# An embedding lookup and interaction tower on one core: tables laid out by partition, grams transposed straight from PSUM, and a new order of steps

## What is computed

```python
e = jnp.stack([tbl_0[ids[:, 0]], ..., tbl_25[ids[:, 25]]], axis=1)      # (512, 26, 128)
all_emb = jnp.concatenate([bottom_output[:, None, :], e], axis=1)       # (512, 27, 128)
gram = jnp.einsum('bfd,bgd->bfg', all_emb, all_emb)
z = gram[:, _TRIU_I, _TRIU_J]                                           # 351 pairs
h = jnp.concatenate([z, bottom_output], axis=1)
h = jnp.maximum(h @ W_top1 + b_top1, 0.0)                               # 479 -> 512
h = jnp.maximum(h @ W_top2 + b_top2, 0.0)                               # 512 -> 256
y = h @ W_top3                                                          # 256 -> 1
```

## Time and profile before

| | us |
|---|---|
| median of 3 runs | 102.84 (102.78 to 103.25) |
| profiled execution, first to last instruction | 100.5 |
| TensorE (PE) busy | 95.8, 95% |
| weight loads (PEld) busy | 83.0, 83% |
| VectorE (DVE) busy | 66.4, 66% |
| ScalarE (ACT) busy | 58.1, 58% |
| GpSimd (POOL) busy | 60.6, 60% |

### The profile page before, as it was taken

How to read it: one execution, slowest core, us unless ns; L and a number is a source line. 1 busy time by engine, 2 the same in 40 slices (tenths; PEclk the granted TensorE clock), 3 DMA queues, 4 the chain that set the end, 5 groups by cost and what they waited for, 6 DMA issues and landing times.

```text
span 100.5 us, 3571 instructions
## 1 busy us (share of the span) xinstructions
PE 95.8 (95%) x1512; PEld 83.0 (83%) x1512; DVE 66.4 (66%) x164; ACT 58.1 (58%) x97; POOL 60.6 (60%) x64
## 2 busy tenths in 40 slices
PE   3999999999999999999999998999999999899992
PEld 3798687888888888888979987889989989798980
DVE  2499999999999999989797009206630681078001
ACT  5556959958996999994945304352433345312341
POOL 2678777787787787777777777777777700000000
DMA  2999979999999999999982221222222200000000
GB/s 46 265 267 263 198 222 243 227 224 232 217 193 216 231 233 232 221 219 245 252 249 85 52 59 52 59 59 52 59 59 52 62 26 7 0 7 0 1 7 0
DMA packets 6544, 13.55 MB, mean 135 GB/s; under 512 B 2076, under 2 KB 2860, under 8 KB 6528
## 3 DMA queue, kind: packets, MB, share of 16 engines
q1 hardware_dynamic: 4536, 9.51, 40.6%
q0 software_dynamic: 1824, 3.74, 15.6%
q10 hardware_dynamic: 168, 0.07, 0.3%
HBM read 13.30 MB, written 0.01 MB: 132 GB/s over the span
## 4 chain that ended last, share of the span: by engine, by line
PE 86%; DMA 5%; ACT 3%; SPq 2%; issue 1%; ACTq 0%
PE acc L663 34%; PE acc L729 12%; PE acc L763 12%; PE acc L691 8%; PE ring L703 6%; PE ring L774 5%; DMA raw<-tbl 5%; PE acc L754 4%; SPq L299 2%; PE ring L737 1%; PE ring L787 1%; ACT hi L376 1%; PE ring L798 1%; ACT onehot L420 1%; ACT emb L461 1%
## 5 line engine op out<-in xcount | busy, mean ns | idle before, releaser
L359 POOL DMA_INDIRECT rows<-tbl,ids_sb x57 | 59.9, 1050 | 18.7 <-issue 17.1
L547 DVE TENSOR_SCALAR onehot<-far 125x512 fp32r<-125x512 f32 (+2 forms) x92 | 32.2, 408 | 1.6 <-ACT far L390 1.6
L663 PE MATMUL acc<-onehot,hi 125*128 125x512 f32 (+1 forms) x84 | 23.8, 406 | 0.2 <-ACT onehot L420 0.2
L663 PE MATMUL acc<-onehot,lo 125*128 125x512 f32 (+1 forms) x84 | 22.3, 390 | 0.0
L663 PEld LDWEIGHTS acc<-onehot,lo 125*128 125x128 f32 x84 | 16.1, 193 | 3.0
L663 PEld LDWEIGHTS acc<-onehot,hi 125*128 125x128 f32 x84 | 15.5, 195 | 3.7 <-DVE onehot L547 0.6
L533 DVE TENSOR_TENSOR lo<-raw,hi 125x512 fp32r<-125x512 f32 (+1 forms) x24 | 16.8, 701 | 0.6 <-ACT hi L376 0.5
L568 DVE COPY gram<-acc 128x432 f32<-128x432 f32 x4 | 3.7, 915 | 19.8 <-PE acc L729 19.8
L376 ACT CAST hi<-raw 125x1024 fp32r<-125x1024 f32 (+1 forms) x11 | 12.0, 1090 | 7.0 <-DMA raw<-tbl 2.9
L729 PE MATMUL acc<-emb 128*27 128x27 f32 x1024 | 12.6, 193 | 0.9 <-ACT emb L461 0.4
L729 PEld LDWEIGHTS acc<-emb 128*27 128x27 f32 x1024 | 10.7, 104 | 3.4 <-issue 1.4
(11 more groups left out here) (53 smaller groups left out, 84.2 us busy)
## 6 DMA issues: line engine op xcount, KB each, us to landing
raw<-tbl SPq DMA_DIRECT2D x9, 448.0 KB
raw<-tbl SPq DMA_DIRECT2D x2, 560.0 KB
ids_b<-ids SPq DMA_DIRECT2D x4, 256.0 KB, 10.5
rows<-tbl,ids_sb POOLq DMA_INDIRECT x57, 8.3
w1z<-w SPq DMA_DIRECT2D x3, 234.0 KB
w_sb<-w SPq DMA_DIRECT2D x1, 512.0 KB
raw<-tbl SPq DMA_DIRECT2D x9, 52.0 KB
raw<-tbl SPq DMA_DIRECT2D x2, 224.0 KB
```

Source lines behind the costliest of these rows:

```text
L359: nc.gpsimd.indirect_dma_start(out=rows[:, t, slot, :], out_offset=None, in_=tables[table], in_offset=bass.IndirectOffsetOnAxis(ap=ids_sb[ ...
L547: ins = nc.vector.tensor_scalar(onehot[:, n % OH_RING, k, of], far[:, t % FAR_RING, of], float(c), None, ALU.is_equal)
L663: mm = nc.tensor.matmul(acc[:, look_bank(t), 0:looked_up(t)], part_of[:, t % HL_RING, c * D:(c + 1) * D], onehot[:, n % OH_RING, k, 0:look ...
```

## The change

Two changes at once.

Tables. The host hands each small table over in a new layout: row c x 128 + p of the table stands on partition p as chunk c (128 partitions, padded with repeated rows to 1024 or 1280). far becomes |id - p| in ScalarE's one operation, so the one-hot of chunk 0 is relu(1 - far), one operation and no `away`; chunk c > 0 is where far equals 128 c. ScalarE makes chunk 0 for every table but the first, and chunk 1 too for tables 1 and 2 (`SECOND`), that one over |far - 128|. A table is one DMA, and table 2's load is issued after table 0 has landed.

Grams. The two copies to SBUF are gone: VectorE transposes from the two PSUM banks that hold a tile's products, with a stride of 27 elements. `pairs` has two buffers; a tile's first gram waits until both transposes of the tile before have read the banks (`pairs_ready`). Two banks hold grams, four layer 1. `ORDER` is new behind the lookups: nine runs of grams in place of twelve, and other places for bottom, turn, l1 and columns.

```diff
-KP = 125
+KP = 128
-GPS = 3
-TOP = 3
+GPS = 2
+TOP = 4
+SECOND = (1, 2)
...
-    return GPS + (n + 1) % TOP
+    return GPS + (n + 2) % TOP
...
-    return 0 < j < NL - 2 and (paired(j) or j >= FIRST)
+    return 0 if j == 0 else 2 if j in SECOND else 1
...
-                table = tables[LOOKED_UP[j]].rearrange("(p k) d -> p (k d)", k=chunks(j))
-                for p0, p1 in ((0, SPREAD), (SPREAD, KP)):
-                    sp.dma_start(raw[p0:p1, j % RAW_RING, c0 * D:c1 * D],
-                                 table[p0:p1, c0 * D:c1 * D]).then_inc(landed, 16)
+                table = looked[j]
+                sp.dma_start(raw[:, j % RAW_RING, c0 * D:c1 * D], table[:, c0 * D:c1 * D]).then_inc(landed, 16)
...
             load_rows(1, 0, chunks(1), raw_in[1])
+            sp.wait_ge(raw_in[0], 16)
             load_rows(2, 0, chunks(2), raw_in[2])
...
-                nc.scalar.activation(far[:, j % FAR_RING, 0:looked_up(j)], of, ACT.Identity,
-                                     bias=neg_row[:, c:c + 1]).then_inc(far_ready, 1)
+                nc.scalar.activation(far[:, j % FAR_RING, 0:looked_up(j)], of, ACT.Abs,
+                                     bias=neg_row[:]).then_inc(far_ready, 1)
...
-                        nc.scalar.activation(away[:], far[:, t % FAR_RING, :], ACT.Abs).then_inc(away_ready, 1)
...
-                        nc.scalar.activation(onehot[:, n % OH_RING, 0, :], away[:], ACT.Relu,
+                        nc.scalar.activation(onehot[:, n % OH_RING, 0, :], far[:, t % FAR_RING, :], ACT.Relu,
+                                             bias=1.0, scale=-1.0).then_inc(oh_act, 1)
+                    if 0 < t < HL_RING:
+
+                        split(t)
+                    if by_act(t) > 1:
+                        if SECOND.index(t):
+
+                            act.wait_ge(oh_act, act_made(t))
+                        nc.scalar.activation(away[:], far[:, t % FAR_RING, :], ACT.Abs,
+                                             bias=neg_second[:]).then_inc(away_ready, 1)
+                        act.wait_ge(away_ready, SECOND.index(t) + 1)
+                        nc.scalar.activation(onehot[:, n % OH_RING, 1, :], away[:], ACT.Relu,
                                              bias=1.0, scale=-1.0).then_inc(oh_act, 1)
...
-                    nc.vector.tensor_copy(gram[:, t % 2, :, UNIT:2 * UNIT].rearrange("p g u -> p u g"),
-                                          acc[:, gram_bank(t, 1), 0:UNIT * NF].rearrange("p (u g) -> p u g", g=NF)
-                                          ).then_inc(cut_dve, 1)
...
-                    nc.vector.transpose(pairs[:, 0:NF - 1, :], gram[:, t % 2, 1:NF, :]).then_inc(pairs_ready, 1)
-                    nc.vector.transpose(pairs[:, NF - 1:, :], gram[:, t % 2, 0:DELTAS, :]).then_inc(pairs_ready, 1)
+                    grams = acc[:, 0:UNITS, 0:UNIT * NF].rearrange("p n (u g) -> p g n u", g=NF)
+                    nc.vector.transpose(pairs[:, t % 2, 0:NF - 1, :].rearrange("p g (n u) -> p g n u", n=UNITS),
+                                        grams[:, 1:NF]).then_inc(pairs_ready, 1)
+                    nc.vector.transpose(pairs[:, t % 2, NF - 1:, :].rearrange("p g (n u) -> p g n u", n=UNITS),
+                                        grams[:, 0:DELTAS]).then_inc(pairs_ready, 1)
...
+                            pe.wait_ge(pairs_ready, 2 * t)
```

and of the list, its last lines:

```diff
-              ("turn", 3, 3), ("bottom", 2, 0), ("pairs", 2, 0), ("gram", 3, (0, 20)), ("bottom", 2, 1), ("l1", 2, 0),
-              ("l1", 2, 1), ("gram", 3, (20, 32)), ("l1", 2, 2), ("l1", 2, 3), ("l2", 2, 0), ("bottom", 3, 0),
+              ("l2", 1, 0), ("turn", 3, 2), ("bottom", 2, 1), ("turn", 3, 3), ("pairs", 2, 0), ("gram", 3, (0, 20)),
+              ("l1", 2, 0), ("l1", 2, 1), ("l1", 2, 2), ("gram", 3, (20, 32)), ("l1", 2, 3), ("l2", 2, 0),
```

More of the change, by code:

```diff
@@ L172, in by_act, with tower @@
 def by_act(j):
-    return 0 < j < NL - 2 and (paired(j) or j >= FIRST)
+    return 0 if j == 0 else 2 if j in SECOND else 1
 def act_made(j):
-    return sum(by_act(i) for i in range(j + 1))
+    return sum(by_act(i) for i in range(j))
 def turn_count(t, g):
     return TURNS * t + g + 1
-def tower(nc, bottom, ids, ids_t, ids_16, tables, w1, b1, w2, b2, b2_row, w3, w3_row, out):
+def tower(nc, bottom, ids, ids_t, ids_16, tables, looked, w1, b1, w2, b2, b2_row, w3, w3_row, out):
     ctx = ExitStack()
@@ L201, in tower @@
             pass
-        gram = sb("gram", [128, 2, NF, U])
-        pairs = sb("pairs", [128, NF - 1 + DELTAS, QP])
+        pairs = sb("pairs", [128, 2, NF - 1 + DELTAS, QP])
         zt = sb("zt", [ZK, 2, ZC, LANES])
@@ L370, in split @@
                     each = chunks(0) // 2 * D
-                    act.wait_ge(raw_in[0] if half else first_raw_in, 32)
+                    act.wait_ge(raw_in[0] if half else first_raw_in, 16)
                     part = slice(half * each, (half + 1) * each)
@@ L471, in _ @@
                                    ).then_inc(emb_turned, 1)
-                elif step == "gram":
-                    if not part[0] < UNIT <= part[1]:
-                        continue
-                    if t >= 2:
-                        act.wait_ge(pairs_ready, 2 * (t - 1))
-                    act.wait_ge(gram_done, t * UNITS + 1)
-                    nc.scalar.copy(gram[:, t % 2, :, 0:UNIT].rearrange("p g u -> p u g"),
-                                   acc[:, gram_bank(t, 0), 0:UNIT * NF].rearrange("p (u g) -> p u g", g=NF)
-                                   ).then_inc(cut_act, 1)
                 elif step == "pairs":
@@ L543, in _ @@
                             dve.wait_ge(oh_used, n - OH_RING + 1)
-                        for k in range(1 if by_act(t) and half == 0 else 0, chunks(t) // 2):
+                        for k in range(by_act(t) if half == 0 else 0, chunks(t) // 2):
                             c = half * chunks(t) // 2 + k
                             of = slice(0, looked_up(t) if t < NL - 2 else PART)
-                            ins = nc.vector.tensor_scalar(onehot[:, n % OH_RING, k, of], far[:, t % FAR_RING, of], float(c),
+                            ins = nc.vector.tensor_scalar(onehot[:, n % OH_RING, k, of], far[:, t % FAR_RING, of], float(KP * c),
                                                           None, ALU.is_equal)
@@ L579, in _ @@
                         dve.wait_ge(pairs_done, t)
-                    start = pairs[:, 0, 0:1]
+                    start = pairs[:, t % 2, 0, 0:1]
                     picked = bass.AP(start.tensor, start.offset, [list(start.ap[0]), [QP + 1, NF], [QP, DELTAS]])
@@ L834 @@
     ids_16_d = nc.dram_tensor("ids_16", (NL, B), I16, kind="Internal").ap()
-    tables_d = [given(f"tbl_{i}", inputs[f"tbl_{i}"]) for i in range(TABLES)]
+    tables_d = {i: given(f"tbl_{i}", inputs[f"tbl_{i}"]) for i in GATHERED + LOOKED_UP[:1]}
+    looked_d = []
+    for j, i in enumerate(LOOKED_UP):
+        table = np.asarray(inputs[f"tbl_{i}"])
+        table = table[np.minimum(np.arange(KP * chunks(j)), table.shape[0] - 1)]
+        looked_d.append(given(f"looked_{i}", table.reshape(chunks(j), KP, D).transpose(1, 0, 2).reshape(KP, -1)))
     w1_d = given("w1", w1[order])
```

82 lines of the change are left out of this document (32 added, 50 removed), and 7 rows, old and new, of the table behind.

## The result

The changed kernel takes 101.61 us (median of 20 runs, 101.02 to 102.39), the kernel before 102.59 on the same chip; the ratio is 0.9916 (95% interval 0.9895 to 0.9937), 0.86 us faster by the ratio and 0.98 by the medians. Medians are of all executions; ratios and intervals leave out those more than 1.5% above the fastest of their kernel, which are three of six of `grams_only`, its profiled one among them, three of eleven of `old_order` and at most two of any other. The profiled execution spans 100.2 us against 100.5.

A forecast was written before the change was run, and what follows sets the result against it. The prediction took TensorE as the bound, with GpSimd's gathers right behind. It took 0.7 us up to turn (3,3) and 0.8 behind it, gave 0.1 back, and forecast 102.84 - 1.4 = 101.5 us, 8-in-10 range 101.0 to 102.9.

The forecast's parts named there:

- Startup: First table lookups on TensorE: 0 to 0.7 us won by 17.7, then lost waiting for gathers at turn (0,1); 0.1 taken.
- ScalarE costs nothing: During the lookups: nothing charged for ScalarE's changed one-hot work, since it has gaps and its operations fall from 16 to 15.
- Gram runs and stalls: TensorE's grams before turn (3,3): nine runs for twelve at 0.26 each, -0.8 us; half the 1.1 us of stalls gone, -0.5.
- L461: TensorE's wait for ScalarE's copy ahead of gram 1: hidden by steps now placed between them, -0.4 us.
- the bottom steps: Both bottom steps of tile 2 move ahead of turn (3,3), 0.45 us each: +0.9 us before that turn.
- T: Start of turn (3,3), which reads the last gathers: 82.19 before, forecast 81.5, 0.7 us sooner (0.4 to 1.1).
- three switches fewer: Part of a gram run's cost: 0.19 us extra for passes ahead of a gram, saved in three runs.
- The gathers: GpSimd's last gather lands at 81.4 after 0.15 us gained from fewer VectorE operations, slightly later than TensorE's 81.3.
- the second rival: Gram stalls don't shrink, or grow, so TensorE and not the gathers sets turn (3,3), at 82.2 or later: 102.2; chance 0.1.
- From T to the end: Turn (3,3) to the end: 15.84 us falls to about 15.1, -0.8, from bottom steps moved and a gram copy dropped.
- The disputed price: VectorE's transposes reading PSUM 27 elements apart: taken as today, 1.05 and 0.57 us; upper bound 1.0 us more per tile.
- rival 1: Strided PSUM reads by VectorE's transposes cost 2.1 ns an element, 1.0 us exposed in tile 3: 102.5; chance 0.2.

The follow-up runs named there:

- grams_only: The gram part and the new step list alone, tables as in the kernel before: 102.96 us over six executions, ratio 0.9891 from three of them.
- old_order: The changed kernel with the kernel before's list of steps put back, table part and PSUM transposes kept: 102.31 us, ratio 0.9924 to the kernel before.
- cut_runs: The changed kernel with its two runs of 160 gram passes cut into 80 and 80, other steps between: 101.15 us, ratio 0.9842.
- tables_only: The table part alone, grams and step list as in the kernel before: 102.64 us, ratio 0.9983.
- after_again: The changed kernel run once more, nothing altered, for a second profile and a comparison in the same stretch of runs: 101.72 us.
- bottom_back: The changed kernel with one pair of bottom passes (tile 2, second half) behind turn (3,3) in place of ahead of it: 101.35 us, ratio 0.9874.
- shifted: The changed kernel with two of three warm-up products replaced by 32 tiny ones, moving later TensorE instructions along the stream: 106.24 us, ratio 1.0317.
- padded: The changed kernel with 112 waits on a long-set semaphore (56 instructions) ahead of TensorE's first product: 112.25 us.

## Why the prediction came out, and which steps failed

The time, 101.61 for 101.5, and the sign are right; half of the working is not, and part of the match is luck. The forecast took 1.34 us off a median of 102.84; the measured gain is 0.86 to 0.98, and the kernel before came out at 102.59.

**Startup** (up to 0.7 won by 17.7, absorbed at turn (0,1), 0.1 taken). Nothing was won in this profile, and for a reason that I had not priced: table 2, whose load waits for table 0, landed at 11.6. In the five profiles in which it landed by 10.8, turn (0,0) came at 16.8 to 16.9, so the 0.7 and a little more were won there. And the absorption is wrong: turn (0,1) never waits, so where the start gained, it was passed on (turn (0,1) at 21.8 in `cut_runs`).

**ScalarE costs nothing.** Wrong by 0.3 to 0.5 us: the one-hot of the last table came late for its part step (0.98 us for four passes in place of 0.64 in the changed kernel's profile, a wait of 0.5 in `tables_only`). And at the start TensorE waits 0.6 for the second one-hot of table 2.

**Gram runs and stalls** (-0.8 and -0.5). This is the step that failed. The gram passes of tiles 0 to 2 take 10.9 us in the seven runs of the changed kernel (the rows above) and 10.05 in the ten of before, six of which are these (the other four, of 64 and 32 passes, take 0.77, 0.42, 0.74 and 0.42):

```profile
55.43 1.15 PE L729 MATMUL acc<-emb 128*27 128x27 f32 x96
...
58.62 1.53 PE L729 MATMUL acc<-emb 128*27 128x27 f32 x96
...
66.57 1.78 PE L729 MATMUL acc<-emb 128*27 128x27 f32 x128
...
70.49 1.10 PE L729 MATMUL acc<-emb 128*27 128x27 f32 x96
...
74.16 1.19 PE L729 MATMUL acc<-emb 128*27 128x27 f32 x96
...
77.69 0.95 PE L729 MATMUL acc<-emb 128*27 128x27 f32 x64
```

Runs without a stall of 160, 128, 96, 64 and 32 passes take 1.53, 1.27, 1.00, 0.73 and 0.42; against these the stalls are 3.2 us after and 1.75 before (the waits view, which lists only part of them, has 2.1 and 1.4 for all four tiles). The three runs fewer were real, and the stalls took 1.4 more where I had taken 0.5 less. I had counted runs and not asked what a run costs that outlasts the supply of instructions. The page of the profile put them down to "issue", which I took for something that fewer runs would lessen.

**L461** (-0.4) and **the bottom steps** (+0.9): right. In all, turn (0,1) to T took 60.15 us in place of 59.48, where I had 0.8 less. These terms (0.9 for the gram passes, -0.4, +0.9, 0.3 for the part step) would give 1.7 more and not 0.7: some 1 us went outside the gram passes, where I had three switches fewer at 0.19, and no row takes it apart.

**The gathers.** The last was issued at 78.67 (78.9 forecast, 79.08 before), but T was TensorE's, as the second rival has it. The agreement proves little: in `after_again`, the same kernel, the last was issued at 79.03, and in `bottom_back`, with the same work on VectorE, at 77.82. The forecast had called 0.3 us real by the Trainium skill's rule on VectorE's and GpSimd's port (SBUF - State Buffer, the section on its two separate sides), and 0.4 came; no run takes it apart.

**From T to the end** (-0.8): -0.83. Turn to gram -0.10, gram 3 with what lies between its runs -0.09, last gram to pairs 3.62 to 2.69 (2.68 forecast), pairs to l1 +0.11, l1 to l3 with columns +0.18 (0.15 forecast). That T was late took nothing from it. But misses cancel in this sum. Gram 3's stretch was to grow by 0.2 (an l1 step of 0.67 more, a bottom step of 0.45 less) and shrank by 0.1, as the stall at place 2754 was 0.3 shorter in this profile than in that of before. Against it, turn to gram and pairs to l1 each took 0.1 more than forecast.

**The disputed price.** 1.05 and 0.57 us, the lower bound: a stride of 27 elements in PSUM costs a VectorE transpose nothing. The Trainium skill, Advanced Engine Details and Errata, section Memory Cachelines, would have every two consecutive elements together, and by it rival 1 (1.0 us more in each tile); for this operation the trace does not agree.

The profiles alone would say -0.2 at the last layer; the runs say -0.86. Each timed execution on record is 1.7 to 1.8 us longer than its own span, so the profiled one of before, 100.5, took about 102.3 by estimate, under the median of 102.59, and the changed kernel's, at 101.99, is over its own of 101.61. Of the 2.3 us that I had put down to what lies around the span, some 0.5 was thus the profiled execution lying under the median. The executions compared are single ones, in which the landing of table 2 (10.0 to 12.0) and the stalls at 2243 and 2755 (0 to 0.9 each) move the end by as much as the change does. That the number came out so near though T did not come sooner in the profile is in part chance.

## What to carry to other kernels

A stall put down to "issue" inside a dense run of tiny instructions can be the supply of instructions, as the long ones here were: see whether it returns at the same place of the stream and how long the same run takes elsewhere, before counting on fewer, longer runs. Cutting runs of 160 passes at 80 took 0.9 us off the runs themselves, of which little was left further on; so look at the whole stretch, and look again after any edit that adds instructions ahead. Before a step is moved, look whether it covers a wait for something other than what the profile names.

## What was not expected of the hardware

- 56 satisfied waits moved on TensorE took 5.7 us, 0.1 each, and moved stalls of up to 2.5 us into gram runs that had no long ones.
- After 2.2 us of standing still TensorE was granted 0.51 in the next 2 us of `shifted` (88 to 90), 0.64 in the two behind them and 1.00 from 92 on; in `padded`, after 2.46 us, it stayed at 1.00.
- Tables loaded by one DMA over 128 partitions in place of 112 and 13: the DMA engines' share fell from 0.97 to 0.73 over the same stretch at the same rate (224 and 228 GB/s), and gathers landed 3.9 us after issue (median) in place of 8.3. `tables_only` has 0.73 and 3.8, `grams_only` 0.96 and 7.7, so it belongs to the table part. The windows of the changed kernel:

```profile
3.00:55.35 52.35, 51.53 (x347) 43.71 (x347) 47.66 (x127) 39.81 (x60) 41.01 (x38) 1.00 0.73 228
```

No run separated the DMAs' shape from the new layout of the tables.
